# The second layer's one-block chunk moves from the end to the start, and the last stage's work is spread over the tiles of a full chunk

## The reference

```python
x = x + ffn0(cond0(x))         # layer 0: state space convolution, then a SwiGLU of 1792 hidden columns
x = x + ffn1(cond1(x))         # layer 1, below

def cond1(x):                  # per sequence, rows of A and B chosen by its index
    gate = x @ W_gate.T + 0.5 * B_gate(A_gate(x))
    up   = x @ W_up.T   + 0.5 * B_up(A_up(x))
    act  = silu(gate) * up                       # 1376 hidden columns
    return act @ W_down.T + 0.5 * B_down(A_down(act))

def ffn1(y):
    xn = y * rsqrt(mean(y * y) + eps)
    xq = clip(round(xn * s), -128, 127) / s      # s = 127 / max|xn| of the row
    wq = clip(round(W / m), -1, 1) * m           # m = mean|W|
    return y + gelu(xq @ wq.T + b)
```

## Time and profile before

| | us |
|---|---|
| three runs | 1141.06, 1136.92, 1140.66; median 1140.66 |
| profiled execution, its own time | 1140.98 |
| its span, first to last instruction | 1139.1 |
| PE busy | 1065.4 (94%) |
| DVE busy | 556.1 (49%) |
| ACT busy | 307.1 (27%) |
| POOL busy | 134.4 (12%) |

### The profile page before, as it was taken

One profiled execution on the slowest core, in us unless ns is written; L12 is line 12 of the kernel. 1 busy time (PEld: TensorE's weight loads), 2 busy tenths in 40 slices (PEclk: granted clock), 3 DMA queues, 4 the chain that ended last, 5 costly groups with the idle time before them and its releaser, 6 DMA issues.

```text
span 1139.1 us, 13740 instructions
## 1 busy us (share of the span) xinstructions
PE 1065.4 (94%) x5448; PEld 896.1 (79%) x5448; DVE 556.1 (49%) x680; ACT 307.1 (27%) x489; POOL 134.4 (12%) x178
## 2 busy tenths in 40 slices
PE   1899999999999999999889999999999999988775
PEld 0788888888888888888778888888888888877652
DVE  8855454444343444434753343343343344357876
ACT  1522121212112121212432131131131131134665
POOL 4400000000000000000140010010010010024325
PEclk9899999999999999999999999999999999998887
DMA  3776010100101010010411031030030130032103
GB/s 104 238 249 234 2 56 1 55 0 0 55 0 55 0 55 0 21 71 1 148 61 42 28 100 38 28 108 31 28 110 28 28 110 28 28 110 76 45 1 148
DMA packets 25425, 71.81 MB, mean 63 GB/s; under 512 B 5235, under 2 KB 5427, under 8 KB 25267
## 3 DMA queue, kind: packets, MB, share of 16 engines
q1 hardware_dynamic: 19762, 46.24, 11.5%
q0 software_dynamic: 5632, 25.17, 7.2%
HBM read 67.06 MB, written 4.34 MB: 63 GB/s over the span
## 4 chain that ended last, share of the span: by engine, by line
PE 86%; DVE 8%; ACT 2%; issue 2%; DMA 1%; POOL 0%; DVEq 0%; ACTq 0%; POOLq 0%
PE ps_gu L137 18%; PE ps_gu L138 18%; PE ps_gu L139 18%; PE ps_d L137 8%; PE ps_d L138 8%; PE ps_d L139 8%; PE ps_t L139 1%; PE ps_t L138 1%; PE ps_t L137 1%; PE ps_gu L837 1%; DVE h_lo L1626 1%; PE ps_t L728 1%; DVE ar_lo L1443 1%; ACT a_hi L1001 1%; ACT z_new L1091 1%
## 5 line engine op out<-in xcount | busy, mean ns | idle before, releaser
L137 PE MATMUL ps_gu<-a_hi,gu_hi 128*128 128x512 f32 x800 | 316.3, 395 | 2.2 <-DVE a_lo L1312 2.2
L138 PE MATMUL ps_gu<-a_lo,gu_hi 128*128 128x512 f32 x800 | 313.7, 392 | 0.0
L139 PE MATMUL ps_gu<-a_hi,gu_lo 128*128 128x512 f32 x800 | 312.7, 391 | 0.0
L139 PEld LDWEIGHTS ps_gu<-a_hi,gu_lo 128*128 128x128 f32 x800 | 151.1, 189 | 32.4
L137 PEld LDWEIGHTS ps_gu<-a_hi,gu_hi 128*128 128x128 f32 x800 | 151.6, 190 | 31.6 <-DVE a_lo L1312 2.3
L138 PEld LDWEIGHTS ps_gu<-a_lo,gu_hi 128*128 128x128 f32 x800 | 151.7, 190 | 28.4
L1480 DVE TENSOR_TENSOR s_act<-s_act,ps_gu 128x512 f32<-128x512 f32 x44 | 30.2, 687 | 193.7 <-PE ps_gu L139 193.5
L1347 DVE TENSOR_TENSOR s_act<-s_act,ps_gu 128x512 f32<-128x512 f32 x56 | 38.4, 686 | 148.0 <-PE ps_gu L139 148.0
L311 POOL DMA_INDIRECT lr_raw<-in_tab_l,rows x48 | 45.8, 955 | 369.1 <-PE ps_t L728 346.3
L137 PE MATMUL ps_d<-h_hi,dn_hi 128*128 128x512 f32 x224 | 87.6, 391 | 0.0
L139 PE MATMUL ps_d<-h_hi,dn_lo 128*128 128x512 f32 x224 | 87.2, 389 | 0.0
(11 more groups left out here) (244 smaller groups left out, 1707.3 us busy)
## 6 DMA issues: line engine op xcount, KB each, us to landing
raw<-in_w SPq DMA_DIRECT2D x26, 768.0 KB, 5.5
toep_hi<-krev_hi SPq DMA_DIRECT2D x12, 512.0 KB, 5.7
toep_lo<-krev_lo SPq DMA_DIRECT2D x12, 512.0 KB, 6.9
acc<-in_x_t SPq DMA_DIRECT2D x4, 1024.0 KB, 11.1
out<-x1b SPq DMA_DIRECT2D x16, 256.0 KB, 2.0
toep_lo<-krev_hi SPq DMA_DIRECT2D x4, 512.0 KB, 6.1
w_all<-in_wq SPq DMA_DIRECT2D x1, 1024.0 KB, 8.2
raw<-in_wq SPq DMA_DIRECT2D x4, 256.0 KB, 4.0
```

Of the source, the lines that this page charges most:

```text
L137: pe.matmul(out_ap, st_hi, mv_hi, start=start, stop=False, skip_group_check=skip)
L138: pe.matmul(out_ap, st_hi, mv_lo, start=False, stop=False, skip_group_check=skip)
L139: return pe.matmul(out_ap, st_lo, mv_hi, start=False, stop=stop, skip_group_check=skip)
```

## The change

The blocks of layer 1 are put in another order by the host: block 0, the padding, then blocks 1 to 10 (`half_first`). Chunk 7 now holds one block, chunks 8 to 12 two.

Chunk 7 is written out by hand. Its PE order is `half_gate(0)`, `half_up(0)`, and then for each tile `half_gate(t + 1)`, `down_part`, `lora_hidden`, `half_up(t + 1)`; `transposes(t)` stands at the end of `half_up(t)`. DVE copies the first sums to `z` and `td` instead of adding them, and POOL no longer clears these two. Slot 0 of the weights is split for chunk 8 in the last tile of chunk 7, slot 1 is split already at the end of layer 0. Chunks 8 to 11 keep the order that they had.

Chunk 12 has full tiles. During tile t, PE also makes the `bd` rows of tile t - 1 (`lora_rows`), its `x_rows` in two halves between gate 0 and up 0 of tile t + 1, and, for t = 2 and 3, `quantised(t - 2)` and four logit products. Behind the last rank product are `lora_rows(3)`, `quantised(2)`, `x_rows(3)`, `quantised(3)` and products 8 to 15. DVE's `finish` is cut into `fresh`, `largest`, `with_x` (two halves) and `factors`, with `logits` and `whole` put between them. ACT's order is written anew too, with `gelu` in between. POOL does `x_sums(4t - 1, 4t + 3)` and `whole(t - 2)` behind the gathers of tile t. The logits and their GELU lie in four slots of `td` (`Y_SLOT`). The memory for POOL's DMA descriptors is set to 8192 bytes a partition. The tiles of SBUF are laid out anew.

The core of the diff (lines taken out are mostly left out; they stand in the functions above; the splitting and adding functions only change their arguments):

```diff
+                    sp.dma_start(raw[:, f].rearrange("p a n -> p (a n)"), w1[3 * f]).then_inc(s_raw0[f], 16)
+                sp.wait_ge(s_wlg[0], NC0 + 1)
+                sp.wait_ge(s_wld[0], NC0 + 1)
+                sp.dma_start(raw[:, 0].rearrange("p a n -> p (a n)"), w1[2]).then_inc(s_raw0[0], 16)
+                with sp.Fori(NC0 + 1, CL) as c:
...
-                pool.memset(x1b[:], 0.0).then_inc(v_zero, 1)
...
-                pool.memset(td[:], 0.0).then_inc(q_tev, 1)
...
+                def whole(t):
+                    for s in range(4 * t, 4 * t + 4):
+                        if s in ON_VECTOR:
+                            continue
+                        pool.wait_ge(e_gb, s + 1)
+                        pool.wait_ge(e_zx, 2 * t + 1 + s % 4 // 2)
+                        pool.tensor_tensor(z[:, s], z[:, s], y_row(s), ALU.add).then_inc(e_op, 1)
+                pool.wait_ge(s_wlg[1], CL)
+                pool.wait_ge(s_wld[1], CL)
+                lora_down_rows(0)
+                x_sums(0, 2)
+                for t in range(NT):
+                    if t + 1 < NT:
+                        pool.wait_ge(r_bl, RL + t + 1)
+                        pool.wait_ge(r_lt, RL + t + 1)
+                        step(t + 1)
+                    if t == 0:
+                        x_sums(2, 3)
+                    if t:
+                        pool.wait_ge(q_bd, t)
+                        lora_down_rows(t)
+                        x_sums(4 * t - 1, 4 * t + 3)
                     if t >= 2:
+                        whole(t - 2)
+                x_sums(NSUB - 1, NSUB)
+                for t in range(2, NT):
+                    whole(t)
...
+                def down_part(f, c, t, m):
+                    if t == 0:
+                        pe.wait_ge(s_wld[f], c + (1 - f))
+                    pe.wait_ge(s_hl[f], tiles(f, m) + 1)
+                    for s in range(4):
+                        if f == 0 and isinstance(m, int) and m > ML:
+                            pe.wait_ge(e_zx, 2 * (m - ML) - 1 + s // 2)
+                        elif f == 0 and s == 0:
                             pe.wait_ge(s_ev, m)
+                        sl = slice(s * P, (s + 1) * P)
+                        last = mm3(pe, ps_d[:, s], h_hi[:, f, sl], h_lo[:, f, sl], dn_hi[:, f], dn_lo[:, f],
+                                   start=(f == 0), stop=(f == 1), skip=True)
+                    return last
...
+                def half_gate(t):
+                    pe.wait_ge(s_silu[0], M1 + t)
+                    gate_up(ps_gu[0], 0, 0, 0, t, t + 1).then_inc(s_g[0], 1)
+                def half_up(t):
+                    pe.wait_ge(s_mul[0], M1 + t)
+                    gate_up(ps_gu[1], 1, 0, 0, t, t + 1).then_inc(s_u[0], 1)
+                    pe.wait_ge(q_tev, t + 1)
+                    transposes(ps_t, 1, t)
+                pe.wait_ge(c_tm[0], NG // 2)
                 pe.sem_inc(q_td, 1)
+                pe.sem_inc(q_tev, 1)
+                pe.wait_ge(s_wlg[0], NC0 + 1)
+                pe.wait_ge(s_mul[1], M1)
+                half_gate(0)
+                half_up(0)
+                for t in range(NT):
+                    if t + 1 < NT:
+                        half_gate(t + 1)
+                    down_part(0, NC0, t, M1 + t).then_inc(s_d[1], 1)
+                    pe.wait_ge(r_adl, t + 1)
+                    lora_hidden((0,), M1 + t)
+                    if t + 1 < NT:
+                        half_up(t + 1)
+                pe.wait_ge(s_silu[0], M1 + NT)
+                with pe.Fori(NC0 + 1, CL) as c:
                     for t in range(NT):
                         m = c * NT + t
                         r = c * NT + (t - M1)
                         for f in range(2):
                             if t == 0:
+                                pe.wait_ge(s_wlg[f], c + (1 - f))
+                            pe.wait_ge((s_mul, s_silu)[f][1], tiles(1, m))
...
+                def gate_0(t):
                     m = ML + t
                     if t == 0:
                         pe.wait_ge(s_wlg[0], CL + 1)
+                    pe.wait_ge(s_mul[1], tiles(1, m))
+                    gate_up(ps_gu[0], 0, 0, 0, t, RL + t + 1).then_inc(s_g[0], 1)
+                def up_0(t):
+                    m = ML + t
+                    pe.wait_ge(s_mul[0], m)
                     if t == 3:
+                        pe.wait_ge(e_qt, 2)
+                    gate_up(ps_gu[1], 1, 0, 0, t, RL + t + 1).then_inc(s_u[0], 1)
+                pe.wait_ge(s_silu[1], tiles(1, ML))
+                pe.wait_ge(s_wsum, 1)
+                pe.wait_ge(s_id, 5)
+                pe.matmul(ps_gu[2][:, 0:1], ones[:], wsum[:], start=True, stop=True).then_inc(e_wp, 1)
+                gate_0(0)
+                up_0(0)
+                pe.wait_ge(s_wlg[1], CL)
+                pe.wait_ge(e_wm, 1)
                 for t in range(NT):
                     m = ML + t
+                    if t:
+                        pe.wait_ge(s_silu[1], tiles(1, m))
+                    if t == 3:
+                        pe.wait_ge(e_yb, 4)
+                    gate_up(ps_gu[2], 0, 1, 1, t, RL + t + 1).then_inc(s_g[1], 1)
+                    pe.wait_ge(q_tev, RL + t + 1)
+                    transposes(ps_t, 2, RL + t)
+                    pe.wait_ge(s_silu[0], m + 1)
+                    gate_up(ps_gu[0], 1, 1, 1, t, RL + t + 1).then_inc(s_u[1], 1)
+                    if t >= 2:
+                        quantised(t - 2)
+                    if t:
+                        lora_rows(t - 1)
+                    if t >= 2:
+                        pe.wait_ge(e_wq, KB)
+                        product(4 * t - 8)
+                    if t == 3:
+                        product(4 * t - 7)
                     if t + 1 < NT:
+                        gate_0(t + 1)
+                    if t:
+                        x_rows(t - 1, 0)
+                    if t == 2:
+                        product(4 * t - 7)
+                    if t == 3:
+                        product(4 * t - 6)
+                    if t + 1 < NT:
+                        up_0(t + 1)
+                    if t:
+                        x_rows(t - 1, 1)
+                    if t == 2:
+                        product(4 * t - 6)
+                    if t == 3:
+                        product(4 * t - 5)
+                    down_part(0, CL, t, m)
+                    if t == 2:
+                        product(4 * t - 5)
+                    down_part(1, CL, t, m).then_inc(s_d[1], 1)
                     pe.wait_ge(r_adl, RL + t + 1)
+                    lora_hidden((0, 1), m)
+                lora_rows(3)
                 quantised(2)
+                x_rows(3, 0)
+                product(8)
+                product(9)
+                x_rows(3, 1)
+                product(10)
+                product(11)
                 quantised(3)
+                for s in range(12, NSUB):
+                    product(s)
...
+                b_split(1, 0)
+                gate(0, M1)
+                for t in range(NT):
+                    m = M1 + t
+                    hidden_high(0, m, t)
+                    down_rows(1, t)
+                    act.wait_ge(s_u[0], m + 1)
+                    b_split(1 if t + 1 < NT else 2, t + 1)
+                    if t + 1 < NT:
+                        gate(0, m + 1)
+                    else:
+                        next_gate_up(0, NC0)
+                        act.wait_ge(s_d[1], m + 1)
+                        act.activation(dn_hi[:, 0], raw[:, 0, 2], ACT.Copy).then_inc(s_whd[0], 1)
+                with act.Fori(NC0 + 1, CL) as c:
...
                     if t:
+                        td_high(t - 1)
+                    hidden_high(0, m, r)
+                    gate(1, m)
+                    down_rows(2, r)
+                    hidden_high(1, m, r)
+                    if t >= 2:
+                        keep_quantised(t - 2)
                     if t + 1 < NT:
+                        act.wait_ge(s_u[1], tiles(1, m) + 1)
+                        b_split(2, r + 1)
                     if t:
+                        squares(t - 1)
+                    if t + 1 < NT:
+                        gate(0, m + 1)
+                    if t:
+                        roots(t - 1)
+                    bd_split(t)
+                    if t == 3:
+                        for s in range(4, 6):
+                            gelu(s)
+                    if t == 2:
+                        gelu(0)
+                        gelu(1)
+                    if t in (1, 2):
+                        scaled(t - 1)
+                    if t == 2:
+                        gelu(2)
+                        gelu(3)
+                    if t in (1, 2):
                         to_bf16(t - 1)
...
+                gelu(6)
+                scaled(2)
+                td_high(3)
+                gelu(7)
+                to_bf16(2)
+                keep_quantised(2)
+                squares(3)
+                roots(3)
```

(83 more changed lines are left out.)

501 lines of the change are left out of this document (192 added, 309 removed).

## The result

The changed kernel takes 1157.36 us (median of 4 runs, 1156.36 to 1158.77) against 1140.14 us of the kernel before beside it (1136.92 to 1141.06). The ratio is 1.0157, 95% interval 1.0133 to 1.0181: slower. The forecast was 1154.5 with a range of 1136 to 1165.

What follows compares the result with a forecast made beforehand. PE was taken as the bound, saturated in full chunks. Start 585.8, half chunk 71.8, full chunks 338.9, last chunk 120.3 and tail 35.9 gave a 1152.7 span; with 1.9 around it and a small adjustment, 1154.5 us, range 1136 to 1165.

Steps and rivals of the forecast that it cites:

- The half chunk, 71.8 forecast: First chunk of the layer: 42.4 us of PE work, 21.0 for three stops, 8.4 at the boundary to full chunks.
- The stops of 5.1: Half chunk, tiles 1 to 3: PE waits for `b_lo`, a chain of 7.83 us less 2.72 of gate cover.
- the 4.5 for `gu_lo`: Before the first full chunk: PE stops for `gu_lo`, 9.9 us less 2.0 of SwiGLU stop and 3.44 of work.
- Clock behind a stop: Half chunk: slow granted clock after each PE stop costs 1.9 us on the mean, from three earlier windows.
- The last chunk, 120.3 forecast: Last chunk with full tiles: 107.6 us of PE work plus 12.7 of stops and slow clock, listed by tile.
- 1.35 + 1.65: Last chunk, tile 1: 1.35 us for `with_x(0)` queued behind other DVE work, 1.65 for DVE held up by POOL's sums.
- the 1.4 for `with_x(2)` in tile 3: Last chunk, tile 3: a stop for `with_x(2)` behind `whole(3)` and `logits(6)`, 0.5 to 3 us, taken as 1.4.
- The tail, 35.9 forecast: Behind the last chunk: 3.0 us uncovered, 4.6 for `lora_rows(3)`, 28.3 to the end; bounds 31 and 41.
- The 28.3: Tail after `lora_rows(3)`: the earlier 36.6 us to the end, less 2.3 of waiting and 6.0 of products.
- the half chunk without stops: Rival: in the half chunk the gather lands and is split inside 2.72 us, or is covered; 1125 us, chance 0.10.
- The last chunk with 4 us of stops and a tail of 31: Rival: gathers stall as forecast, but the end of the kernel loses less; 1141 us, no change, chance 0.16.
- The bound on DVE and POOL: Rival: DVE, held up by POOL's reads, bounds the last chunk; 3.5 us more in three tiles, 1168 us, chance 0.12.

Runs made afterwards that it cites:

- the early transposes: Changed kernel with half-chunk transposes moved to the free third bank, right behind the gate of their own tile; tried in two versions, 1134.75 us and 1131.46 us.
- the first version: Changed kernel with half-chunk transposes in the third bank, behind the whole gate instead of behind up; 1134.75 us, ratio 0.9956 to the kernel before.
- the second: The first version with transposes between gate products and low-rank part, later bank wait, down rows ahead of hidden values; 1131.46 us, ratio 0.9936.

## Why the prediction held

The measured time lies 2.9 us above the forecast, and by the profile each large term is near. Some luck is in the sum: in the span, which is 1.8 above the forecast, an earlier start hides 2.0 of the 3.8 that the half chunk (0.3), the last chunk (1.6) and the tail (1.9) took more than forecast.

- **Start of the layer.** I took 585.8 from the trace of before; it was 583.77. POOL's first gather for the layer's projections already starts 2.1 us earlier, in work that the change does not touch, and other versions with the same start have the first gate at up to 585.99, so this is scatter and no gain of the change.
- **The half chunk, 71.8 forecast, 72.13 measured.** The stops of 5.1 were 5.34, 5.03 and 5.15; the 2.0 for the SwiGLU of tile 3 was 1.95; the 4.5 for `gu_lo` was 4.13. Clock behind a stop was put at 1.9 and is 1.8 on the mean. That the sum is met to 0.3 is in part chance, since this chunk measures 71.3 to 74.0 where its code is the same. The mechanism was tested from both sides: the gather buffer let go sooner took the stops away, a delay on POOL made those on `b_lo` longer by nearly its length. What I did not see is that tile 1 differs from tiles 2 and 3 when the transposes are early; it made no difference in the forecast.
- **The rule of the Trainium skill on the cost of a gather** (DMA: Bandwidth & Descriptors, Anatomy of one DMA — SWDGE) gives an estimate of 2.9 us and would have the stops 1.3 us shorter. The second gather's start to the split was 4.34 us here and the stops were 5.03 to 5.34, so the rows of before were the better guide.
- **The full chunks, 338.9:** 338.90.
- **The last chunk, 120.3 forecast, 121.93 measured.** The stops that I listed came nearly all: 0.85 was 0.78, 1.3 was 1.43, 0.85 was 1.05, 0.6 was 0.86, 0.6 was 0.64, 2.05 was 1.98. For tile 1 I had 1.35 + 1.65 = 3.0 and 1 of clock; it was 2.88 and 1.7. The runs show that the 2.88 is order and contention together: without POOL's sums 0.86 of it stays, with the z sum ahead of the factors nothing. So the order's part was 0.86 and not 1.35, POOL's part 2.0 and not 1.65. One item was wrong: the 1.4 for `with_x(2)` in tile 3 did not come. It came only when logits were put ahead of the maxima. Clock was undersized: 2 us in the forecast; 121.93 - 107.6 - 9.6 leaves 4.7 for it and for small gaps, 1.7 of it behind the 2.88 (0.66 over 5 us) and 1.65 behind the 1.98 (0.67 over 5 us). The two errors, 1.0 too much of stops and 2.7 too little of clock and gaps, partly cancel.
- **The tail, 35.9 forecast, 37.77 measured.** 3.0 was 3.06 (to 1119.79); `lora_rows` 5.5 to the start of `fresh(3)`, not 4.6, on a clock of 0.50; and from there to the end 29.2, not 28.3. The 28.3 was taken from the end of before less what goes, and did not count that `keep_quantised(2)` stands before the squares (0.45) and that a row sum of POOL stretches the clip, 2.50 for 1.43, for which the last copy to bf16 waited 0.32. These terms were mis-sized by 0.9 each.
- **Slips in the working.** "Four logit products are about 0.95" is one product of four matmuls; the sum uses it rightly. The PE work behind 1010.4 adds up to 79.1, not 79.2. The bounds of the half chunk come out of their own terms at 68.6 and 74.8, not 67.5 and 76. None of it moves the forecast.

The rivals: the half chunk without stops is refuted, and the early transposes show what it would have been worth, 20.8 us of half chunk in the first version and 24.4 in the second, of the 29.4. The last chunk with 4 us of stops and a tail of 31 did not come. The bound on DVE and POOL did not come either; contention was there but cost the path 2.0 us and some clock in one tile, and 0.3 in the tail.

**The ledger.** Last chunk and tail hold 84.7 us of tile work and 36.8 of the last stage (rows of `bd`, `x_rows`, `quantised` and logit products, as the prediction priced them), 121.5 in 159.7, so 38.2 are stops and slow clock; before they were 49.5. The cover for norm, residual and product is there and gives 11.3. The half chunk loses 29.7, where the kernel before lost 1.0 in its five full chunks, since it had hidden the gathers of its half tiles behind the last stage. 29.7 + 38.2 - 49.5 - 1.0 = 17.4, less the 2.0 of the earlier start: 15.4, the difference of the two spans. The forecast's ledger had 64.1 where 67.9 came.

## What to carry to other kernels

When a short tile is moved to another place, look at the buffers that pass from tile to tile: a chain of a fixed length (here 7.8 us from release to split) is hidden by a long tile and bare beside a short one, and the cure here was to release the buffer earlier. A second buffer or a faster transfer was not tried. Count for each stop what runs slow behind it, here a third of the stop again for stops of 4 to 5 us. When most of the stops went, only about half of the slow clock went with them (3.8 of 7.1 us with the early transposes), since the stops of about 2 us that were left had slow stretches behind them too. In the timeline of an engine that is not the bottleneck, look for tiny operations with long durations, and before moving their neighbour try to move the result that PE waits for ahead of them.
